# An expert-tile loop with row transposes three turns ahead, down products three turns behind and triple-buffered product inputs

## The reference

```python
x = x + attn(layernorm(x))            # 16 heads, causal window of 64, Wq Wk Wv Wo
z = layernorm(x)
scores = sigmoid(z @ gate_w.T + lb_bias)          # 8 experts
topw, topi = top_k(scores, 2); topw /= topw.sum(-1)
for e in range(8):                                # expert: 256 -> 128 -> 256
    sel   = (topi == e).any(-1)
    wmean = (topw * (topi == e)).sum() / count(topi == e)
    out += where(sel, mlp(z, gate[e], up[e], down[e]) * wmean, 0)
out += mlp(z, shared_gate, shared_up, shared_down)   # 256 -> 256 -> 256
x = x + out                            # mlp = silu(z @ g.T) * (z @ u.T) @ d.T
```

## Time and profile before

| | us |
|---|---|
| median of 3 runs | 596.92 |
| lowest and highest | 594.46, 598.95 |
| the profiled execution | 591.49 |
| its span, first to last instruction | 589.7 |
| expert tiles, first to last `hidden_T` | 403.2 to 532.9 |
| mean granted PE clock | 0.962 of 2.4 GHz |

### The profile page before, as it was taken

The page is one execution under the profiler, slowest core; times in us unless marked ns, Lnnn a source line. Parts: engine busy times, 40 slices in busy tenths (PEclk is TensorE's granted clock), DMA queues, the critical chain, the costliest instruction groups (busy, mean ns, idle before and its releaser), DMA issues.

```text
span 589.7 us, 16243 instructions
## 1 busy us (share of the span) xinstructions
PE 521.1 (88%) x5573; PEld 431.5 (73%) x5573; DVE 414.3 (70%) x1299; ACT 315.9 (54%) x736; POOL 222.4 (38%) x384
## 2 busy tenths in 40 slices
PE   7699989999988998999999877888889889789997
PEld 4567777777777776787677546787788887678996
DVE  6566788788888888888887763655555665552675
ACT  3566666665765766666576422314566665653111
POOL 4000011253154145225314427622555555453651
PEclk8899999988999999998999975989999999999999
DMA  8500101212212231221112033586444444434994
GB/s 261 188 2 4 38 4 38 83 39 84 83 42 79 83 94 46 83 82 39 55 57 74 32 127 115 178 209 220 140 138 146 145 142 135 133 107 135 400 399 154
DMA packets 42751, 67.96 MB, mean 115 GB/s; under 512 B 9772, under 2 KB 28847, under 8 KB 42672
## 3 DMA queue, kind: packets, MB, share of 16 engines
q1 hardware_dynamic: 34128, 42.72, 23.3%
q0 software_dynamic: 6528, 16.86, 8.3%
q10 hardware_dynamic: 2016, 7.34, 3.6%
HBM read 36.02 MB, written 31.66 MB: 115 GB/s over the span
## 4 chain that ended last, share of the span: by engine, by line
PE 70%; DVE 19%; issue 5%; ACT 3%; another core or an unknown queue 1%; DMA 1%; SPq 0%; POOL 0%; ACTq 0%; DVEq 0%; POOLq 0%
PE ps L524 37%; PE ps L583 6%; PE ps L612 5%; PE ps L767 5%; DVE rmax L1115 4%; PE ps L837 3%; PE ps L594 3%; DVE stats L1096 2%; PE ps L620 2%; PE ps L578 2%; DVE xs L1145 2%; PE ps L599 2%; PE ps L535 2%; PE ps L854 2%; PE ps L650 2%
## 5 line engine op out<-in xcount | busy, mean ns | idle before, releaser
L524 PE MATMUL ps<-wF,wA 128*128 x648 | 106.8, 303 | 10.4 <-DVE wA L1413 7.1
L524 PEld LDWEIGHTS ps<-wF,wA 128*128 128x128 f32 x648 | 85.7, 189 | 20.3 <-issue 18.4
L509 POOL DMA_INDIRECT y_rows<-vm,dest x72 | 70.4, 978 | 79.6 <-ACT vm L1068 32.9
L1115 DVE TRANSPOSE_TENSOR_REDUCE rmax<-ps 128x32 f32<-128x1024 f32 x64 | 79.3, 1239 | 10.0 <-PE ps L583 9.9
L937 ACT ACTIVATE probs<-ps 128x1024 f32<-128x1024 f32 x64 | 65.6, 1024 | 36.0 <-PE ps L599 35.6
L413 POOL TENSOR_TENSOR rstd<-mv,epsb 128x2 f32<-128x2 f32 x32 | 6.4, 201 | 207.2 <-DVE mv L1100 206.2
L469 POOL DMA_INDIRECT z_slots<-z,slot x64 | 64.7, 1010 | 28.2 <-issue 16.9
L524 PE MATMUL ps<-yT,wA 128*128 128x256 f32 x384 | 69.2, 314 | 1.6 <-DVE yT L1090 1.5
L583 PE MATMUL ps<-bd,kT 64*128 64x256 f32 x512 | 69.9, 395 | 0.0
L524 PEld LDWEIGHTS ps<-yT,wA 128*128 128x128 f32 x384 | 55.4, 204 | 5.2 <-issue 2.9
L583 PEld LDWEIGHTS ps<-bd,kT 64*128 64x128 f32 x512 | 51.6, 198 | 5.7
(11 more groups left out here) (183 smaller groups left out, 1157.0 us busy)
## 6 DMA issues: line engine op xcount, KB each, us to landing
z<-z_slots SPq DMA_DIRECT2D x72, 129.0 KB
zT_scratch<-zT SPq DMA_DIRECT2D x16, 512.0 KB
bd<-y_rows SPq DMA_DIRECT2D x8, 512.0 KB, 10.7
out<-xs SPq DMA_DIRECT2D x16, 256.0 KB, 7.5
wraw_of<-wffn SPq DMA_DIRECT2D x10, 384.0 KB, 3.8
xs<-x SPq DMA_DIRECT2D x7, 512.0 KB, 6.6
wA<-zT_scratch ACTq DMA_DIRECT2D x7, 512.0 KB, 6.2
shift<-negs SPq DMA_DIRECT2D x128, 2.0 KB
```

The source lines that it names most:

```text
L509: eng.indirect_dma_start(y_rows, bass.IndirectOffsetOnAxis(ap=dest[:, m:m + 1], axis=0), yo[:, m, :], None, bounds_check=K * T - 1, oob_is ...
L524: mm = eng.matmul(out, lhsT(a), rhs(b), start=start and n == 0, stop=stop and n == 2, skip_group_check=skip)
L1115: eng.tensor_reduce(rmax[:, n % 2, 0:32], S[n % 2].rearrange("p a (c q) -> p (a c) q", q=32), AX.X, ALU.max, apply_transpose=True).then_in ...
```

## The change

Three things, all in the stage of the expert tiles.

- **Order.** In turn t the PE does `rows_T(t+3)`, `tile_gate_up(t+1)`, `hidden_T(t-1)`, `tile_down(t-3)`. ACT and DVE follow in the same order: `rows_hi(t+3)`, `silu(t+1)`, `hidden_hi(t-1)`, `scaled(t-3)`, and `rows_lo(t+3)`, `hidden(t+1)`, `hidden_lo(t-1)`, `destinations(t+1)`. The first and last turns are written out to match; at the end the gate and up products of unit 10 stand before the last two down products.
- **Buffers.** `z1`, `h1` and `hT` have three buffers each (two small new tensors and 512 columns of `wA` that were free in this stage). The waits that guard them look one tile further back. PSUM stays at two banks of each kind, and the four waits on the banks are the same tile for tile.
- **The load of the expert numbers** (`experts_of`) moves from the second turn of each eight to the fourth.

No instruction is added or taken away.

```diff
-        z1 = wAflat[:, 0:2 * 2 * D].rearrange("p (b a c) -> p b a c", b=2, a=2)
-        hT = wAflat[:, 2048:2048 + 2 * 2 * P].rearrange("p (b a c) -> p b a c", b=2, a=2)
+        z1 = [wAflat[:, c:c + 2 * D].rearrange("p (a c) -> p a c", a=2) for c in (0, 2 * D, 3584)]
+        hT = [wAflat[:, c:c + 2 * P].rearrange("p (a c) -> p a c", a=2) for c in (2048, 2048 + 2 * P)] + [hT_2]
...
-        h1 = vtflat[:, 1536:1536 + 4 * P].rearrange("p (a b c) -> p a b c", a=2, b=2)
+        h1 = [vtflat[:, c:c + 2 * P].rearrange("p (b c) -> p b c", b=2) for c in (1536, 1536 + 2 * P)] + [h1_2]
...  PE
                 def tile(q, m, first, last):
-                    if not (last and m >= 6):
-                        rows_T(*later(q, m, 2))
+                    if not (last and m >= 5):
+                        rows_T(*later(q, m, 3))
                     if not (last and m == 7):
                         tile_gate_up(*later(q, m, 1))
-                    if m == 1 and not last:
+                    if m == 3 and not last:
                         experts_of(q + 1)
-                    hidden_T(*later(q, m, 0))
                     if not (first and m == 0):
-                        tile_down(*later(q, m, -1))
+                        hidden_T(*later(q, m, -1))
+                    if not (first and m < 3):
+                        tile_down(*later(q, m, -3))
...
+                rows_T(2, 0, 2)
                 sweep_tiles(eng, tile)
+                hidden_T(NTS - 1, NTS // 8 - 1, 7)
+                tile_down(NTS - 3, NTS // 8 - 1, 5)
                 eng.wait_ge(s_h1, NTS)
                 gate_up(NS * GA)
+                tile_down(NTS - 2, NTS // 8 - 1, 6)
                 tile_down(NTS - 1, NTS // 8 - 1, 7)
...  ACT
-                    after(eng, s_g1, t - 1)
+                    after(eng, s_g1, t - 2)                      # rows_hi
-                    after(eng, s_h1, t - 1)
+                    after(eng, s_h1, t - 2)                      # silu
-                    after(eng, s_d1, t - 1)
+                    after(eng, s_d1, t - 2)                      # hidden_hi
...
-                    hidden_hi(*later(q, m, 0))
                     if not (first and m == 0):
-                        scaled(*later(q, m, -1))
+                        hidden_hi(*later(q, m, -1))
+                    if not (first and m < 3):
+                        scaled(*later(q, m, -3))
...  DVE
-                    after(eng, s_hT, t - 1)
+                    after(eng, s_hT, t - 2)                      # hidden
...
-                    hidden_lo(*later(q, m, 0))
-                    destinations(*later(q, m, 0))
+                    if not (first and m == 0):
+                        hidden_lo(*later(q, m, -1))
+                    if not (last and m == 7):
+                        destinations(*later(q, m, 1))
```

More of the change, by code:

```diff
@@ L844, in tile_gate_up @@
                     for k in range(KT):
-                        mm = product(ps[:, m % 2, 0:2 * P], lambda a: z1[:, m % 2, a, k * P:(k + 1) * P],
+                        mm = product(ps[:, m % 2, 0:2 * P], lambda a: z1[t % 3][:, a, k * P:(k + 1) * P],
                                      lambda b: weights(e, b, 2 * k * P, 2 * (k + 1) * P), k == 0, k == KT - 1)
@@ L1051, in _ @@
                                   ).then_inc(zt_of[g][1], 16)
+                rows_hi(2, 0, 2)
                 def silu(t, q, m):
                     eng.wait_ge(s_g1, t + 1)
-                    after(eng, s_h1, t - 1)
-                    eng.activation(h1[:, m % 2, 0, :], ps[:, m % 2, 0:P], ACT.Silu).then_inc(s_s1, 1)
+                    after(eng, s_h1, t - 2)
+                    eng.activation(h1[t % 3][:, 0, :], ps[:, m % 2, 0:P], ACT.Silu).then_inc(s_s1, 1)
                 def hidden_hi(t, q, m):
                     eng.wait_ge(s_hT, t + 1)
-                    after(eng, s_d1, t - 1)
-                    eng.copy(hT[:, m % 2, 0, :], ps[:, 6 + m % 2, 0:P]).then_inc(s_hTh, 1)
+                    after(eng, s_d1, t - 2)
+                    eng.copy(hT[t % 3][:, 0, :], ps[:, 6 + m % 2, 0:P]).then_inc(s_hTh, 1)
                 def scaled(t, q, m):
@@ L1070, in tile @@
                 def tile(q, m, first, last):
-                    if not (last and m >= 6):
-                        rows_hi(*later(q, m, 2))
+                    if not (last and m >= 5):
+                        rows_hi(*later(q, m, 3))
                     if not (last and m == 7):
                         silu(*later(q, m, 1))
-                    hidden_hi(*later(q, m, 0))
                     if not (first and m == 0):
-                        scaled(*later(q, m, -1))
+                        hidden_hi(*later(q, m, -1))
+                    if not (first and m < 3):
+                        scaled(*later(q, m, -3))
                 silu(0, 0, 0)
@@ L1080, in _ @@
                 sweep_tiles(eng, tile)
+                hidden_hi(NTS - 1, NTS // 8 - 1, 7)
+                scaled(NTS - 3, NTS // 8 - 1, 5)
+                silu_of(NS * GA)
+                scaled(NTS - 2, NTS // 8 - 1, 6)
                 scaled(NTS - 1, NTS // 8 - 1, 7)
-                for i in range(NS * GA, NS * NG):
+                for i in range(NS * GA + 1, NS * NG):
                     silu_of(i)
@@ L1336, in tile_places @@
                     chain(eng.tensor_copy(tile_e[:, :], ps[:, BANK_B, 64:64 + NTS]))
-                    eng.memset(h1[:, 0, 0, 0:1], 0.0).then_inc(s_tab, 1)
+                    eng.memset(h1[0][:, 0, 0:1], 0.0).then_inc(s_tab, 1)
                 def token_weights():
@@ L1433, in tile @@
                 def tile(q, m, first, last):
-                    if not (last and m >= 6):
-                        rows_lo(*later(q, m, 2))
+                    if not (last and m >= 5):
+                        rows_lo(*later(q, m, 3))
                     if not (last and m == 7):
                         hidden(*later(q, m, 1))
-                    hidden_lo(*later(q, m, 0))
-                    destinations(*later(q, m, 0))
+                    if not (first and m == 0):
+                        hidden_lo(*later(q, m, -1))
+                    if not (last and m == 7):
+                        destinations(*later(q, m, 1))
                 rows_lo(0, 0, 0)
@@ L1443, in _ @@
                 hidden(0, 0, 0)
+                rows_lo(2, 0, 2)
+                destinations(0, 0, 0)
                 sweep_tiles(eng, tile)
+                hidden_lo(NTS - 1, NTS // 8 - 1, 7)
                 def combined(g):
```

14 lines of the change are left out of this document (8 added, 6 removed).

## The result

The changed kernel takes 600.04 us (median of 20 runs, 597.43 to 603.33), the kernel before 597.08 beside it (20 runs); the ratio is 1.0057, interval [1.0037, 1.0077]. On another chip, later, it was 592.82 against 591.57, ratio 1.0014 [0.9982, 1.0047]. Forecast was 577.

The account below looks back on a forecast made before the run. It took PE to bound the kernel, waiting 27.1 us in the expert tiles on held reports. A gain of 19.8 less 0.3 us at the ends gave -19.5, so 577 from the median 596.9; forecast 570 to 584, 8 in 10 569 to 592.

Parts of the forecast that it names:

- The bound: Expert tiles: PE is busiest, its weight loads idle 27.1 of 125 us; a turn without waits takes 1.41 us.
- The cause: Expert tiles: PE's completion reports are held while POOL issues an indirect DMA, seen 1.27 and 1.81 us late.
- sum over the waits: Expert tiles: 45% to all of 27.1 us idle time goes; half and half gives a gain of 19.8 us.
- free lateness: How late a PE report may come before PE stands still; gate product to hidden_T: 0.53 us before, 1.94 after, bank 1.15.
- Rival A: Expert tiles: PSUM banks and bunched DMAs keep more of the loss; gain only 4 to 12 us, 589 as middle; chance 0.18.
- Other engines: Expert tiles: ACT 1.14, DVE 1.06, POOL 1.28 us a tile, all under 1.41; POOL is the next bound.
- Destinations: DVE's destinations, a turn earlier, wait for an indirect DMA; 3.5 of 6.0 us needed, so costed at nothing.
- rival C: Rows out land late, DVE stands in destinations and PE behind it; 614 us at a chain of 8 us; chance 0.08.
- The ends: After the last tiles: the last indirect DMA may start up to 0.9 us later; 0.3 us lost, between 0 and 1.
- Rival B: Expert tiles: the PE array itself needs 1.83 us a turn, nothing gained, 597 within 3; chance 0.12.

Follow-up runs that it names:

- the run at 1.58: Changed kernel with one 384-column memset on POOL behind each indirect DMA, shortest distance 1.58 us: 585.02 us, ratio 0.9892 to the kernel before.
- the runs at 1.34: Four one-column memsets on POOL behind each indirect DMA: 597.72 us (ratio 1.0007) on the kernel before, 600.89 us (1.0068) on the changed kernel.

## Why the prediction was wrong

**The bound** was read rightly: 27.1 us of idle weight loads, and a turn of 1.41 without waits. Without held reports the tiles took 104 to 107 us, inside the forecast's 105 to 118 or just under.

**The cause, PE's reports held by POOL's indirect DMAs,** was read rightly from two places of the timeline. Taking away only the indirect form took the lateness away. Why the one delays the other is open.

**The step that failed is the sum over the waits.** It took the holds as lengths given from outside, 1.27 and 1.81 us as seen before, set the new free lateness of 1.15 to 1.94 us against them, and counted 73% of 27.1 us as won. (0.66 of 1.28 is 52%, not 55%; that changes nothing.) What was measured instead: 26.0 of the 27.1 us of idle time stayed, 27 silus came over 1 us late instead of 12, and the worst 3.51 late instead of 2.26. The holds are part of a loop: a held report holds the `scaled`, that holds the DMA, the finished tiles pile up, and when they are let go their DMAs follow at 1.28 us and hold the next reports for longer. With the down product three turns behind there are three tiles to pile up, and bunches of three are what the trace shows. The holds grew to 2.4 us regularly and to 3.5 at most, past every free lateness that the change bought. That they grew is measured. That the bunches make them grow is inferred, from the bunches in the timeline and from the run at 1.58, where breaking them took 9.4 us off the turns; the runs at 1.34 don't bear it out. The text's last sentence named this case ("the held reports grow longer as the PE runs on") but gave it no chance and no price. Rival A came nearest in mechanism, with "two DMAs 1.28 apart can hold one through both", and still had it end at a gain.

**A limit that the sum didn't have:** in the changed kernel the PE stops 12 times inside a product (two starts over 0.4 us apart, where 0.16 is usual), 6.1 us in all; in 9 of the 12 it goes on within 0.1 us of a late start on ACT, with up to six finished pieces of work unreported. Of the kernels looked at for it, all those with the down product three turns behind and a distance of 1.17 to 1.34 show this (5 to 12 times each); with one or two turns behind, or with a distance of 1.58, none does. It looks as if the PE can run only so far ahead of its reports. That was argued from the coincidence, not shown by a run of its own.

**Other engines.** POOL's 1.28 was named as the next bound, right as a price but taken as harmless. ACT and DVE at 1.1 us a tile followed easily. **Destinations** at nothing: right; DVE is never idle before L1443, and rival C's mechanism didn't occur. POOL's 25.5 us of waiting for them, in the whole stage, look like the same held chain, since DVE's queue stands behind the late split.

**The ends** were sized at 0.3 us (0 to 1). The two profiles differ, from the first transposes to the end, by 195.1 - 189.7 = 5.4 us: 2.0 because the first `hidden_T` comes a turn later, which the closing turns don't give back while the turn isn't faster; 0.2 in the turns; 3.3 behind the last `hidden_T` (56.7 to 60.1, less rounding). Of that, 1.9 are the drain, in the timeline and the busy time by window of the changed kernel at its end:

```profile
539.74 0.52 PE L526 MATMUL ps<-wF,wA 128*128 x3
...
540.10 0.50 PE L526 MATMUL ps<-wF,hT 128*128 x3
...
541.79 0.84 ACT L1076 ACTIVATE vm<-ps,tile_w 128x256 f32<-128x256 f32 x2 [1.07 <-PE ps L526]
...
542.69 2.37 PE L526 MATMUL ps<-wA,wF 128*128 128x256 f32 x12 [2.08 <-issue]
...
544.86 2.46 PE L526 MATMUL ps<-yT,wF 128*128 128x256 f32 x12
```
```profile
543.00:547.00 4.00, 4.00 (x23) 4.00 (x22) 0.42 (x1) 0.38 (x1) 1.96 (x2) 0.57 0.22 44
536.00:543.00 7.00, 3.94 (x27) 3.44 (x28) 1.68 (x6) 3.66 (x11) 3.92 (x4) 1.00 0.19 68
```

The down product before the last ends at 540.26 (539.74 + 0.52), its report comes 1.5 us late, together with that of the last, under DMAs 1.28 apart, and unit 11 starts at 542.69: 5.2 us behind the last `hidden_T`, against 3.3 before. The other 1.5 us are the clock: in the busy time it was granted at 0.57 from 543 to 547, near its level of 1.2 GHz, after the PE had worked 3.94 of the 7 us ahead of it, so that the next three starts of the PE (542.69, 544.86, 547.15) span 4.5 us, where before they spanned 3.0 at full clock. The medians differ by 3.0 us, not by the 7.9 of the two profiled executions; 2.5 of these lie ahead of the tiles, where nothing was changed.

**Rival B's time, 597, was nearest** to the result, but for a reason that isn't its own. The time alone would have confirmed the wrong mechanism.

The Trainium skill ("Perfetto Trace Analysis", Optimization Strategy) says that the same gap repeating on the busiest engine can mean too little SBUF or PSUM for the next tile. Here SBUF wasn't what was missing: a third buffer for every input left 26.0 of 27.1 us idle, and distance between DMAs of another engine took a third of the gaps away (24.4 of 124 us to 15.8 of 115). More PSUM banks weren't tried.

## What to carry to other kernels

When a stall's length comes from another engine's instructions, and those instructions are released by the stalled work, it is a loop: deeper queues can lengthen the stall instead of covering it. Look whether the holder is paced by the held, and break it there (spread the holder's instructions) before buying slack. And do the cheapest test first: take the holder out altogether, in both orders, to see what the depth alone is worth (here 0.3 to 2.5 us).

## What the runs showed of the hardware

- An indirect DMA issued by POOL (0.98 us; 0.87 with a quarter of the rows) delays the reports of finished matmuls to ACT; a plain DMA issued by POOL or SP doesn't. With 1.28 us as their shortest distance `scaled` came up to 3.35 us late in the changed kernel, with 1.34 up to 3.98, with 1.58 up to 2.55, with 2.08 never over 0.04 (up to 1.21 in the kernel before). Why is open.
- Chips differ in it: beside sixteen of the eighteen runs the kernel before took 591 to 597 us, beside two, on one chip, 560.99, and there no report was late at distances of 1.58 and 1.87. The same kernel with the distance of 1.58 had 32 silus over 1 us late on another chip, so it is the chip that differs and not the distance. Whether that chip never holds reports, and what the change is worth on it, wasn't run.
